# Edge features of a graph layer as three bf16 planes in one product, and loads for four groups at once

## The chip, the cores and the metric
One core of one Trainium2 chip. Time is device microseconds for one launch. The kernel before took 7721.66 us, the median of 3 runs (7720.5 to 7730.41).

## The reference, cut to what matters
12,500 nodes with 48 features, 400,000 edges sorted by target node, 16 features on each edge. Two layers, each with a residual. The first is a normalised graph convolution. The second, which the change touches, is a message network on edges:

```
h = relu(layernorm(x))
edge = concat(h[src], h[dst], edge_feat)           # 48 + 48 + 16
h1 = relu(edge @ W1 + b1)                          # 128
h2 = relu(h1 @ W2 + b2)                            # 128
message = h2 @ W3 + b3                             # 48
update = segment_sum(message, dst) / max(count, 1)
x = x + h + update
```

## The kernel before, in words
A first part (to about 2730 us) builds tables, does the graph convolution and writes p_tab and q_tab to HBM: for each node its share of the first layer, h @ W1[0:48] and h @ W1[48:96], each as three bf16 planes of 128 (768 bytes a row). The bf16 planes add up to nearly the f32 value.

The edge stage follows, and the change lies in it. The edges are padded to 401,408 = 784 groups (NG) of 512 (W = GROUP x P = 4 x 128). For group q:

- SyncE loads, for two groups at a time, source indices (idx), the edges' places within the target window (rel, broadcast to 96 partitions) and 16 rows of f32 edge features (ef, 16 of 128 partitions; the other 112 were cleared once, by memset, line 1454), and for each group 96 rows of q_tab (q_win, 32 nodes x 3 planes). A pair's loads wait until the first layer is done for all but 6 groups (`wait_past(sp, z1_made, q - (DEPTH - 2))`, DEPTH = 8).
- GpSimd gathers 4 x 128 rows of p_tab by four indirect DMAs (line 1362) into p_got, which has 4 buffers (UNROLL): it waits for the pair's loads and for z1_made to reach q - 3.
- VectorE makes two one-hots: hot_t (96 x 512, line 1530; it has two buffers and so waits for the first layer of group q-2) and hot_d (line 1534). ScalarE copies hot_d to bf16 (hot_c, line 1473).
- TensorE makes the first layer z1 (H x 512 in PSUM, two buffers) by the edge part (line 1322: w1c_sb, f32, 128 rows of which 112 are zero, 512 columns, recorded as two passes), the source part (line 1328: 12 bf16 products of 128 columns) and the target part (line 1495: one bf16 product of 96 rows and 512 columns, whose end tells z1_made).
- ScalarE applies bias and relu (h1, line 1348), TensorE multiplies by W2 (line 1334), VectorE keeps the maximum (h2, line 1352), TensorE sums by node (lines 1341 and 1343) and VectorE adds the sums up (lines 1357, 1358).

The order on TensorE is written out: in step q the first layer of q, the second layer of q-1, the sums of q-2. All five engines run a loop over 8 groups (`paced`), with one body per group, and meet only at semaphores. After the stage come rare extra groups (targets outside the 32-node window; `each_extra`) and a closing part with W3 and the division.

Of the kernel before, what the change touches and what calls it, by code (L numbers as in the profile page):

```python
# [17 lines left out]
P = 128  # L18
GROUP = 4
# [33 lines left out]
def paced(eng, steps, body, unroll=UNROLL):  # L53
# [6 lines left out]
    for s in range(unroll):  # L60
        body(steps - unroll + s, s)

# [66 lines left out]
def build_gnn(nc, x, src_col, dst_col, dst_row, edge_t, w0_t, b0, w1ab, w1c, b1, w2, b2, w3, b3, out):  # L129
# [40 lines left out]
    rel_row = dram("rel_row", [NG, W], BF16)  # L170

# [3 lines left out]
    with ExitStack() as whole:  # L175
# [34 lines left out]
        w1c_sb = sb("w1c_sb", [P, H], F32)  # L210
# [4 lines left out]
        w1c_zero = sem("w1c_zero")  # L215
# [465 lines left out]
        with ExitStack() as life:  # L681
# [10 lines left out]
            with ExitStack() as ctx:  # L692
# [26 lines left out]
                def _(pool):  # L719
                    link = linker(pool, scans)  # L720
                    pool.memset(w1c_sb[:, :], 0.0).then_inc(w1c_zero, 1)
# [21 lines left out]
                def _(sp):  # L743
# [38 lines left out]
                    sp.wait_ge(w1c_zero, 1)  # L782
                    weight(w1c_sb[0:EF, :], w1c)
# [536 lines left out]
        def edge_part(pe, z1, ef):  # L1320

            return pe.matmul(z1[:, :], w1c_sb[:, :], ef, start=True, stop=False, skip_group_check=True)  # L1322
# [44 lines left out]
        with ExitStack() as life:  # L1367
            PAIRS = DEPTH // 2
            PAIR_LOADS = 3
            idx = [sb(f"idx_d{j}", [P, 2 * GROUP], I32, life) for j in range(PAIRS)]  # L1370
            rel = [sb(f"rel{j}", [QR, 2 * W], BF16, life) for j in range(PAIRS)]
# [5 lines left out]
            rel_pairs = rel_row.rearrange("(g two) e -> g (two e)", two=2)  # L1377
# [7 lines left out]
            q_x = sb("q_x", [P, PLANES * H], BF16, life)  # L1385
            hot_x = p_flat[3][:, 0:W].rearrange("p (j e) -> p j e", j=GROUP)
# [10 lines left out]
            with ExitStack() as ctx:  # L1397
                ef_zero = sem("ef_zero", ctx)
                cnt_zero = sem("cnt_zero", ctx)
                pair_loaded = [sem(f"pair_loaded{j}", ctx) for j in range(PAIRS)]  # L1400
# [20 lines left out]
                def half_of(pair, s):  # L1421
                    width = pair.shape[1] // 2
                    return pair[:, s % 2 * width:(s % 2 + 1) * width]

                @block.sync
                def _(sp):
                    sp.wait_ge(ef_zero, 1)
                    sp.dma_start(cnt_acc[:, :], zero_b[:, 0:2 * NPP // P].bitcast(F32)).then_inc(cnt_zero, 16)

# [4 lines left out]
                    def step(q, s):  # L1434
                        if s % 2:
                            return
# [15 lines left out]
                def _(pool):  # L1452
                    for j in range(PAIRS):
                        last = pool.memset(ef[j][:, :], 0.0)
# [340 lines left out]
```

## Time and profile before
| what | value |
|---|---|
| median of 3 runs | 7721.66 us |
| the profiled execution: its span | 7782.5 us |
| TensorE busy, whole span | 6395.9 us (82%) |
| GpSimd busy | 3277.8 us (42%) |
| VectorE, ScalarE busy | 3430.9 us (44%), 1920.4 us (25%) |
| line 1322 (edge part) busy, 1568 passes | 1147.1 us |
| line 1362 (gathers) busy, 3136 of them | 2971.2 us |
| mean granted clock | 0.838 |

The profiled execution's own time is its span, 7782.5 us from first to last instruction; no other figure of it is given. The share of busy time is an average over stages with different limits. Idle time is put down to what ended it: "remote" is a semaphore whose updater the profile doesn't tell, "issue" is time in which the engine waited for nothing that the profile shows. Ends of TensorE's products are modelled, so distances are best taken from start to start.

### The profile page before, as it was taken

Reading aid. Unit: us, or ns where it says so; the run is one execution under the profiler, and the core shown is the slowest. Engines: PE = TensorE matmul, PEld = TensorE weight load, DVE = VectorE, ACT = ScalarE, POOL = GpSimd, SP = SyncE. Lnnn points to the kernel's source line nnn. Section 1 sums busy time; section 2 is a strip of 40 time slices with the busy share of each in tenths; the row PEclk is TensorE's granted clock in tenths of the full one; section 3 lists DMA queues with packets and bytes.
Section 4 is the critical chain, followed back from the end, with each engine's and each line's share of the span. In section 5 each row is a group of like instructions: output and inputs, shape, how many; then the busy total and the mean of one; then the engine's idle time right before and its main releaser. Section 6 shows DMA issues by size and latency. Waiting matters only on the chain. (4 is left out here: it accounts for less than half of the span.)

```text
span 7782.5 us, 170432 instructions
## 1 busy us (share of the span) xinstructions
PE 6395.9 (82%) x52124; PEld 5165.3 (66%) x52125; DVE 3430.9 (44%) x8786; ACT 1920.4 (25%) x3658; POOL 3277.8 (42%) x3414
## 2 busy tenths in 40 slices
PE   4868999999998777878888888888788888788878
PEld 4846878888777656666666666666666666666666
DVE  9989878888884612222222222222222222222222
ACT  1236555555541411111111111111111111111111
POOL 1020010001010255556555555555555555555565
PEclk9989999999999577788777778777878878778787
DMA  6026777777766333333333333333333333333333
GB/s 141 0 61 230 250 236 251 253 249 246 241 231 198 104 90 86 86 86 88 86 86 88 86 86 88 87 86 87 88 86 88 87 86 86 86 88 86 86 88 68
DMA packets 556929, 959.01 MB, mean 123 GB/s; under 512 B 277228, under 2 KB 356302, under 8 KB 556454
## 3 DMA queue, kind: packets, MB, share of 16 engines
q1 hardware_dynamic: 401687, 644.10, 26.4%
q0 software_dynamic: 155136, 313.54, 15.4%
q8 instruction: 62, 1.02, 0.1%
q14 instruction: 44, 0.36, 0.0%
HBM read 682.14 MB, written 275.03 MB: 123 GB/s over the span
## 5 line engine op out<-in xcount | busy, mean ns | idle before, releaser
L1362 POOL DMA_INDIRECT p_got<-p_tab,idx_d x3136 | 2971.2, 947 | 2015.1 <-remote 914.4
L1348 ACT ACTIVATE h<-z,b_col 128x512 f32<-128x512 f32 x784 | 538.7, 687 | 4040.1 <-remote 2909.2
L1352 DVE TENSOR_TENSOR h<-z,nb 128x512 f32<-128x512 f32 x784 | 538.7, 687 | 2169.2 <-remote 1522.9
L1334 PE MATMUL z<-w_sb,h 128*128 128x128 f32 x6272 | 1107.2, 312 | 397.1 <-issue 362.3
L1334 PEld LDWEIGHTS z<-w_sb,h 128*128 128x128 f32 x6272 | 1038.3, 226 | 510.3 <-issue 453.3
L816 PE MATMUL a_ps<-tile_r,pair_l 128*128 128x288 bf16 x6272 | 1228.8, 291 | 172.3 <-issue 84.9
L870 DVE TENSOR_SCALAR tile_r<-iota_r,key_r,dst_i 128x576 bf16<-128x576 f16 x3136 | 1171.2, 429 | 279.2 <-PE a_ps L816 133.7
L837 PE MATMUL out_ps<-gw,a_got 121*128 121x144 bf16 x13716 | 1259.3, 227 | 23.6 <-issue 13.1
L1341 PE MATMUL seg_ps<-hot_d,h 128*128 128x32 f32 x6272 | 965.5, 290 | 377.5 <-issue 374.1
L1341 PEld LDWEIGHTS seg_ps<-hot_d,h 128*128 128x128 f32 x6272 | 949.8, 222 | 428.1 <-issue 425.7
L796 ACT CAST stage<-a_ps 128x576 uint16<-128x576 f32 x1568 | 999.0, 638 | 874.3 <-PE a_ps L816 698.1
L1328 PEld LDWEIGHTS z<-ident_b,p_got 128*128 128x128 bf16 x9408 | 764.9, 117 | 650.1 <-issue 636.1
L1322 PE MATMUL z<-ef,w1c_sb 128*128 128x512 f32 x1568 | 1147.1, 821 | 30.1 <-DMA ef<-in_edge_t 24.1
L837 PEld LDWEIGHTS out_ps<-gw,a_got 121*128 121x128 fp8e4 x13716 | 1015.7, 98 | 152.8 <-issue 40.8
L1328 PE MATMUL z<-ident_b,p_got 128*128 128x128 bf16 x9408 | 841.5, 253 | 19.1 <-issue 9.9
L1357 DVE TENSOR_TENSOR big<-big,seg_ps 128x32 f32 x784 | 147.6, 188 | 1593.1 <-remote 1067.1
L727 POOL DMA_INDIRECT gw<-g_tab,gw_row x144 | 149.8, 1040 | 1601.0 <-PE out_ps L837 1559.7
L816 PEld LDWEIGHTS a_ps<-tile_r,pair_l 128*128 128x128 bf16 x6272 | 565.1, 115 | 310.8 <-ACT stage L796 147.8
L1495 PE MATMUL z<-hot_t_d,q_win 96*128 96x512 bf16 x784 | 360.7, 460 | 22.1 <-issue 21.5
L1322 PEld LDWEIGHTS z<-ef,w1c_sb 128*128 128x128 f32 x1568 | 289.3, 230 | 83.0 <-DMA ef<-in_edge_t 24.8
L1343 PE MATMUL seg_ps<-hot_c,ones_b 128*1 128x32 bf16 x3136 | 219.2, 179 | 150.8 <-issue 150.6
L1530 DVE TENSOR_SCALAR hot_t_d<-rel,node_id 96x512 bf16<-96x512 bf16 x784 | 310.2, 396 | 70.3 <-issue 49.8
(168 smaller groups left out, 3560.9 us busy)
## 6 DMA issues: line engine op xcount, KB each, us to landing
a_got<-a_tab SPq DMA_DIRECT2D x396, 576.0 KB, 4.0
a_tab<-stage SPq DMA_DIRECT2D x392, 576.0 KB
rel<-rel_row SPq DMA_DIRECT2D x392, 192.0 KB
p_got<-p_tab,idx_d POOLq DMA_INDIRECT x3136
ef<-in_edge_t SPq DMA_DIRECT2D x392, 64.0 KB
q_win<-q_tab SPq DMA_DIRECT2D x784, 24.0 KB
a_tab<-big SPq DMA_DIRECT2D x22, 567.0 KB
p_tab<-pq_out SPq DMA_DIRECT2D x14, 672.0 KB, 3.6
```

Source lines behind the costliest of these rows:

```text
L796: act.copy(stage[k][:, i % READ, :].rearrange("p (h e) -> p h e", h=2), a_ps[:, 2 * (i % 2):2 * (i % 2) + 2, 0:PIECE]).then_inc(kept, 1)
L816: last = pe.matmul(a_ps[:, 2 * (i % 2) + h, 0:PIECE], pair_l[i // 2 % 3][:, :, i % 2 * WIN_TILES + j], tile_r[i % 4 * WIN_TILES + j][:, h ...
L837: last = pe.matmul((a_ps if tail == 2 else out_ps)[:, c, b * OUT_F:(b + 1) * OUT_F], a_got[0:ROWS, i, :].bitcast(FP8)[:, (3 * c + b) * P:( ...
L870: dve.tensor_scalar(tile_r[i % 4 * WIN_TILES + j][:, :], iota_r[:, :], key_r[:, bass.ds(t, 1)], key_w[:, bass.ds(t, 1)], ALU.is_equal, ALU ...
L1322: return pe.matmul(z1[:, :], w1c_sb[:, :], ef, start=True, stop=False, skip_group_check=True)
L1328: pe.matmul(out_tile, p_rows[:, j, m * H:(m + 1) * H], ident_b[:, :], start=False, stop=False, skip_group_check=True)
L1334: last = pe.matmul(z2[:, j, :], h1_tile, w2_sb[:, :], start=True, stop=True)
L1341: pe.matmul(seg_ps[:, 0:nodes], h2[:, j, :], hot[:, j, :], start=(j == 0), stop=(j == GROUP - 1))
L1348: return act.activation(h1[:, :], z1[:, :], ACT.Relu, bias=b1_col[:, 0:1])
L1352: return dve.tensor_tensor(h2[:, :, :], z2[:, :, :], nb2[:, :].unsqueeze(1).to_broadcast([P, GROUP, H]), ALU.max)
L1362: pool.indirect_dma_start(p_rows[:, j, :], None, p_tab, bass.IndirectOffsetOnAxis(idx[:, j:j + 1], 0)).then_inc(landed, 16)
L1495: pe.matmul(z1[k][:, :], q_win[s][:, :], hot_t[k][:, :], start=False, stop=True, skip_group_check=True).then_inc(z1_made, 1)
```

## The change
Once, ahead of the stage, the 16 x 128 weights W1c are split into three bf16 planes: plane 0 is the rounded value, plane 1 the rounded rest, plane 2 the rest of that. Copies of the planes are laid on the 128 partitions of w1c_rows so that each edge plane meets the weight planes it needs: rows 0 to 47 meet edge plane 0 with weight planes 0, 1, 2; rows 48 to 95 edge plane 1 with 0, 1, 2; rows 96 to 127 edge plane 2 with 0, 1. The ninth product (2 with 2) sits in 16 more rows of the target part, which has 112 rows now: q_win gets the weight plane below its node rows, hot_t the edge plane below the one-hot.

The edge features are split on chip, 8 groups (a block) at a time, as 128 x 512 tiles: ScalarE rounds (three copies), VectorE subtracts (twice), SyncE saves the three planes to a new table e_tab in HBM and loads them back, with edge plane 0 and 1 to three places each and plane 2 to two and to hot_t. That runs up to two blocks ahead. Loads are for four groups (a set, two buffers) in place of two: six loads and four of node rows; they wait for all but 4 groups in place of all but 6. hot_t has room for 8 groups in place of two, and the wait ahead of it is relaxed. The extra groups keep the f32 product, now with 16 rows. The memsets go.

```diff
-            return pe.matmul(z1[:, :], w1c_sb[:, :], ef, start=True, stop=False, skip_group_check=True)
+            return pe.matmul(z1[:, :], weights, ef, start=True, stop=False, skip_group_check=True)
...
-            PAIRS = DEPTH // 2
-            PAIR_LOADS = 3
-            ef = [sb(f"ef{j}", [P, 2 * W], F32, life) for j in range(PAIRS)]
-            q_win = [sb(f"q_win{s}", [QR, H], BF16, life) for s in range(DEPTH)]
-            hot_t = [sb(f"hot_t_d{k}", [QR, W], BF16, life) for k in range(2)]
+            SET = 4
+            SETS = DEPTH // SET
+            SET_LOADS = 6
+            ER = QR + EF
+            e_rows = [(0, 3 * EF, 3), (3 * EF, 6 * EF, 3), (6 * EF, 8 * EF, 2)]
+            ef = [sb(f"ef{j}", [P, SET * W], BF16, life) for j in range(SETS)]
+            q_win = sb("q_win", [ER, DEPTH, H], BF16, life)
+            hot_t = [sb(f"hot_t_d{j}", [ER, SET * W], BF16, life) for j in range(SETS)]
...
+                    def load_block(n):
+                        sp.dma_start(e_left[:, :], block_view(n)).then_inc(e_loaded, 16)
+                    def save_block(n):
+                        sp.wait_ge(e_rounded, n * PLANES + PLANES)
+                        sp.sem_inc(sp_turns, 1)
+                        for m in range(PLANES):
+                            to = e_tab[m, :, bass.ds(n * (DEPTH * W), DEPTH * W)].rearrange("f (g e) -> f g e", g=DEPTH)
+                            sp.dma_start(to, e_planes[:, m, :]).then_inc(e_saved, 16)
...
-                        wait_past(sp, z1_made, q - (DEPTH - 2))
+                        wait_past(sp, z1_made, q - (DEPTH - SET))
...
+                        if s == 0:
+                            sp.wait_ge(e_saved, r * (16 * PLANES) + 16 * PLANES)
...
+                        for m, (low, high, copies) in enumerate(e_rows):
+                            sp.dma_start(ef[j][low:high, :], e_tab[m, :, cols].unsqueeze(1).to_broadcast([EF, copies, SET * W])
+                                         ).then_inc(set_loaded[j], 16)
+                        sp.dma_start(hot_t[j][QR:ER, :], e_tab[PLANES - 1, :, cols]).then_inc(set_loaded[j], 16)
+                        for i in range(SET):
+                            node_rows(q + i, s + i)
+                        if s == 0 and (not isinstance(r, int) or r + 1 < NG // DEPTH):
+                            save_block(r + 1)
+                            if not isinstance(r, int) or r + 2 < NG // DEPTH:
+                                load_block(r + 2)
...
+                    def round_block(n, m):
+                        if m == 0:
+                            act.wait_ge(e_loaded, n * 16 + 16)
+                            act.sem_inc(any_turn, 1)
+                            wait_past(act, e_saved, n * (16 * PLANES))
+                        else:
+                            act.wait_ge(e_taken, n * (PLANES - 1) + m)
+                        act.copy(e_planes[:, m, :], e_left[:, :]).then_inc(e_rounded, 1)
...
+                        if 1 <= s <= PLANES and (not isinstance(r, int) or r + 2 < NG // DEPTH):
+                            round_block(r + 2, s - 1)
                         act.wait_ge(hot_ready, q + 1)
...
-                        edge_part(pe, z1[k], half_of(ef[s // 2], s))
+                        edge_part(pe, z1[k], w1c_rows[:, :], set_part(ef[s // SET], s))
...
-                        wait_past(dve, z1_made, q - 1)
+                        wait_past(dve, z1_made, q - (DEPTH - 1))
...
+                        if 1 <= s < PLANES and (not isinstance(r, int) or r + 2 < NG // DEPTH):
+                            take_plane(r + 2, s - 1)
```

## Rows read from the trace of the kernel before

**Rows 1.** Windows, the edge stage: window, length, busy us (count), granted clock, DMA, GB/s
```profile
2730.00:7728.00 4998.00, 4020.60 (x27406) 3127.18 (x27407) 1175.33 (x3913) 714.36 (x1568) 2971.16 (x3136) 0.80 0.33 87
```

**Rows 2.** Groups by line, edge stage: count, busy us, mean ns, idle before, releasers
```profile
L1362 POOL DMA_INDIRECT p_got<-p_tab,idx_d x3136 | 2971.2, 947 | 2015.1 <-remote 914.4 <-issue 862.8 <-PE z L1495 232.0
...
L1348 ACT ACTIVATE h<-z,b_col 128x512 f32<-128x512 f32 x784 | 538.7, 687 | 4040.1 <-remote 2909.2 <-PE z L1495 1002.5 <-issue 93.6
```

**Rows 3.** Timeline of TensorE, one calm group: start, length, what, idle before
```profile
5003.22 1.13 PE L1322 MATMUL z<-ef,w1c_sb 128*128 128x512 f32 x2
...
5004.18 0.83 PE L1328 MATMUL z<-ident_b,p_got 128*128 128x128 bf16 x12
...
5004.85 0.38 PE L1495 MATMUL z<-hot_t_d,q_win 96*128 96x512 bf16 x1
5005.07 1.05 PE L1334 MATMUL z<-w_sb,h 128*128 128x128 f32 x8
...
5007.05 1.12 PE L1322 MATMUL z<-ef,w1c_sb 128*128 128x512 f32 x2
```

**Rows 4.** Timeline through a stall and the group after it
```profile
5016.35 0.38 PE L1495 MATMUL z<-hot_t_d,q_win 96*128 96x512 bf16 x1
...
5022.12 0.62 PE L1341 MATMUL seg_ps<-hot_d,h 128*128 128x32 f32 x2 [0.52 <-issue]
...
5027.24 2.08 PE L1322 MATMUL z<-ef,w1c_sb 128*128 128x512 f32 x2
5027.24 0.69 ACT L1348 ACTIVATE h<-z,b_col 128x512 f32<-128x512 f32 x1 [12.15 <-remote]
...
5029.11 1.49 PE L1328 MATMUL z<-ident_b,p_got 128*128 128x128 bf16 x12
...
5033.43 1.12 PE L1322 MATMUL z<-ef,w1c_sb 128*128 128x512 f32 x2
```

**Rows 5.** Timeline of GpSimd: gathers, with the idle time ahead of each
```profile
5002.13 0.94 POOL L1362 DMA_INDIRECT p_got<-p_tab,idx_d  x1 [1.90 <-PE z L1495]
...
5008.74 0.94 POOL L1362 DMA_INDIRECT p_got<-p_tab,idx_d  x1 [1.66 <-remote]
5011.39 0.94 POOL L1362 DMA_INDIRECT p_got<-p_tab,idx_d  x1 [1.70 <-issue]
...
5023.85 0.94 POOL L1362 DMA_INDIRECT p_got<-p_tab,idx_d  x1 [0.30 <-issue]
5028.02 0.94 POOL L1362 DMA_INDIRECT p_got<-p_tab,idx_d  x1 [3.23 <-remote]
...
5040.43 0.94 POOL L1362 DMA_INDIRECT p_got<-p_tab,idx_d  x1 [2.72 <-remote]
...
5047.02 0.94 POOL L1362 DMA_INDIRECT p_got<-p_tab,idx_d  x1 [1.91 <-remote]
...
5059.53 0.94 POOL L1362 DMA_INDIRECT p_got<-p_tab,idx_d  x1 [2.80 <-remote]
```

**Rows 6.** Timeline of SyncE's issues, and the window of a pair's loads beside gathers
```profile
5001.55 0.35 SPq L1441 DMA_DIRECT2D idx_d<-in_src_col  x1
...
5002.66 0.32 SPq L1445 DMA_DIRECT2D ef<-in_edge_t  x1
...
5002.90:5005.40 2.50, 2.50 (x24) 1.81 (x24) 0.97 (x5) 0.00 (x0) 1.89 (x3) 1.00 0.65 179
```

**Rows 7.** Timeline, start of the stage
```profile
2726.29 3.62 POOL L1454 MEMSET ef<- 128x1024 f32 x4 [26.57 <-POOLq L912]
...
2735.86 1.07 POOL L1362 DMA_INDIRECT p_got<-p_tab,idx_d  x1 [5.94 <-DMA ef<-in_edge_t]
...
2752.47 0.68 PE L1328 MATMUL z<-ident_b,p_got 128*128 128x128 bf16 x9 [1.65 <-DMA p_got<-p_tab,idx_d]
...
2754.30 0.22 PE L1328 MATMUL z<-ident_b,p_got 128*128 128x128 bf16 x1 [1.16 <-issue]
```

More of the change, by code:

```diff
@@ L61, in paced, with paced_ahead @@
         body(steps - unroll + s, s)
+def paced_ahead(eng, steps, body, unroll=UNROLL):
+    turns = steps // unroll
+    for s in range(unroll):
+        body(s, s, 0)
+    with eng.Fori(1, turns - 2) as r:
+        for s in range(unroll):
+            body(eng.snap(r * unroll + s), s, r)
+    for t in range(turns - 2, turns):
+        for s in range(unroll):
+            body(t * unroll + s, s, t)
 def wait_past(eng, sem, value):
@@ L1397, in build_gnn @@
             with ExitStack() as ctx:
-                ef_zero = sem("ef_zero", ctx)
                 cnt_zero = sem("cnt_zero", ctx)
-                pair_loaded = [sem(f"pair_loaded{j}", ctx) for j in range(PAIRS)]
+                set_loaded = [sem(f"set_loaded{j}", ctx) for j in range(SETS)]
+                e_loaded = sem("e_loaded", ctx)
+                e_rounded = sem("e_rounded", ctx)
+                e_taken = sem("e_taken", ctx)
+                e_saved = sem("e_saved", ctx)
+                w_rounded = sem("w_rounded", ctx)
+                w_taken = sem("w_taken", ctx)
+                w_placed = sem("w_placed", ctx)
                 q_loaded = [sem(f"q_loaded{s}", ctx) for s in range(DEPTH)]
@@ new lines, in _ @@
+                    load_block(0)
+                    sp.dma_start(cnt_acc[:, :], zero_b[:, 0:2 * NPP // P].bitcast(F32)).then_inc(cnt_zero, 16)
+                    sp.wait_ge(w_rounded, PLANES)
+                    for low, high, copies in e_rows:
+                        sp.dma_start(w1c_rows[low:high, :], w1c_planes[:, 0:copies, :]).then_inc(w_placed, 16)
+                    sp.dma_start(q_win[QR:ER, :, :], w1c_planes[:, PLANES - 1:PLANES, :].to_broadcast([EF, DEPTH, H])
+                                 ).then_inc(w_placed, 16)
@@ L1451, in _ @@
                 @block.gpsimd
                 def _(pool):
-                    for j in range(PAIRS):
-                        last = pool.memset(ef[j][:, :], 0.0)
-                    last.then_inc(ef_zero, 1)
                     def step(q, s):
-                        pool.wait_ge(pair_loaded[s // 2], slot_count(q, s, 16 * PAIR_LOADS))
+                        pool.wait_ge(set_loaded[s // SET], set_count(q, s))
                         pool.sem_inc(pool_turns, 1)
@@ L1468, in _, with step @@
                 def _(act):
-                    def step(q, s):
+                    def round_block(n, m):
[6 more added lines that the diff above has]
+                        act.copy(e_planes[:, m, :], e_left[:, :]).then_inc(e_rounded, 1)
+                    for m in range(PLANES):
+                        wait_past(act, w_taken, m)
+                        act.copy(w1c_planes[:, m, :], (w1c_left if m else w1c_sb)[:, :]).then_inc(w_rounded, 1)
+                    for n in range(2):
+                        for m in range(PLANES):
+                            round_block(n, m)
+                    def step(q, s, r):
+                        if 1 <= s <= PLANES and (not isinstance(r, int) or r + 2 < NG // DEPTH):
+                            round_block(r + 2, s - 1)
                         act.wait_ge(hot_ready, q + 1)
@@ L1494, in first @@
                         pe.wait_ge(q_loaded[s], slot_count(q, s, 16))
[L1495 removed]
+                        pe.matmul(z1[k][:, :], q_win[:, s, :], set_part(hot_t[s // SET], s), start=False, stop=True,
                                   skip_group_check=True).then_inc(z1_made, 1)
```

91 lines of the change are left out of this document (55 added, 36 removed).

## The prediction
> **What bounds the kernel now.** I read first where the time lies, then who is held in that stretch, then the order of events. The edge stage, 784 groups of 512 edges, takes 4998 us of 7782.5 (2730 to 7728), so 6.37 us for a group; TensorE is busy in 4020.6 us of it, at a mean granted clock of 0.80 [rows 1]. That looks like a TensorE bound, and the product that the change shrinks (line 1322) is its dearest. The timeline says it is only half true. In a calm stretch TensorE needs 5007.05 - 5003.22 = 3.83 us for a group [rows 3]. GpSimd issues four gathers for a group, each 0.947 us busy with 0.30 us ahead of it [rows 2, 5]: 4 x 1.247 = 4.99 us. So TensorE at the full clock is already faster than GpSimd, and neither explains 6.37.
>
> The missing time is in stalls. In [rows 4] the last product of a group starts at 5016.35, yet the activation that waits for it alone (its neighbours being done) starts at 5027.24, and in between TensorE starts its queued work piece by piece, with 0.5 us and more of idle time ahead of each that nothing releases ("issue"). GpSimd alone keeps its pace. ScalarE's 2909 us of "remote" waits [rows 2] are the sum of such hold-ups. The stall ends when the gathers do: the last of a run starts at 5023.85, ends at 5024.79, and everything moves again at 5027.2; GpSimd resumes at 5028.02 [rows 4, 5]. I don't know the mechanism. The trace shows only that a stall comes some way into an unbroken run of gathers (here 5 us, from 5011.39 to 5016.35; in others that I followed up to 9), and that it lasts until the run is over and has landed. It comes too where TensorE itself waits for gathers: at the start of the stage GpSimd runs from 2735.86 without a break, TensorE waits for a gather at 2752.47, and is in the steps of a stall (1.16 us of idle time ahead of one product) by 2754.30 [rows 7].
>
> GpSimd breaks off because a gather for group q waits for the first layer of group q-4 (four buffers). From 5002.13 to 5059.53 it does 9 groups, 6.38 us each, as the mean. Its rows with more than the usual 0.30 us of idle time are the six of [rows 5]: three of 1.66 to 1.91 us, most of them where TensorE is slow after a stall, and three of 2.72 to 3.23 us, each the end of a stall. Over the usual gap they make 12.2 us for 9 groups, 1.36 us each: 4.99 + 1.36 = 6.35. So the stage is GpSimd's gathers plus the breaks in them, and the change is worth what it takes from the breaks.
>
> **The change, part by part.**
> Edge product. Two f32 passes (5003.22 to 5004.18, 0.96 us) become one bf16 product of 512 columns, which line 1495 shows: 5005.07 - 5004.85 = 0.22 us [rows 3]. At the lower clock (1.2 GHz, granted 0.5) the f32 passes take 5029.11 - 5027.24 = 1.87 us [rows 4], and the bf16 product, at half the speed, twice 0.22, 0.44 us (an estimate). A group falls from 3.83 to 3.09 us in calm, and from 6.19 (5027.24 to 5033.43) to 4.76 after a stall. That is 0.74 to 1.43 us a group, 580 to 1121 us over 784; as a gain it would count in full only if TensorE set the pace. It doesn't: 4.99 us stands above both new figures.
>
> The breaks. After the change even a slow TensorE group (4.76) is under 4.99, so the three short breaks go: by [rows 5] 1.66 + 1.70 + 1.91 less 0.90 is 4.4 us in 9 groups, 0.48 us a group. But without them GpSimd's runs become longer, and a run over some 5 to 9 us brings a stall whose end costs 2.92 us, 2.62 over the usual gap. How long can a run get? GpSimd may go on for each first layer that TensorE has reported before the stall. Until about 7 us into the run TensorE, resuming slowly, now does two for certain and sometimes a third (first after 1.5 to 2 us, then 4.7, then 3.1). So a run is two or three groups: 4.99 + 2.62/2 = 6.30, or 4.99 + 2.62/3 = 5.86. I take the middle, 6.08: 784 x (6.37 - 6.08) = 227 us less. The bounds of this term: 4.99 + 0.1 (no stalls, -1000 us) and 6.37 (0).
>
> Loads. For four groups at once there are six loads in place of two times three, and the edge planes go out three and two times over. Per group in KB: rel 96 as before, edge rows 32 before, now 131 + 16, and in addition 33 of f32 read and 49 written for the table; with node rows and indices about 154 before and 350 now. Gathers are 393. At 6.1 us that is 122 GB/s against 87 [rows 1]; the same engines moved 179 GB/s in a stretch with both kinds [rows 6]. The mean fits. Cost in the mean 0; the bounds come with the burst (below): 0 to +1.5 us a group. By the Trainium skill's page "DMA: Bandwidth & Descriptors", section "Queues, rings and completion order", each DMA engine takes turns between the queues at packet granularity, which speaks against the change: during a set's 983 KB the gathers would lose part of their share. The sum above has no term for it; rows 6 show 179 GB/s for both together, but not who gave way.
>
> Lead of the loads. SyncE now waits for all but 4 groups instead of all but 6, while GpSimd may start group q at all but 3. If GpSimd is at its greatest lead, the release that lets SyncE load set q also lets it start group q-1, 4.99 us before it needs the set. Six issues at (5002.66 - 5001.55)/2 = 0.56 us are 3.3 us; 983 KB at 179 GB/s, or at the 100 that gathers (98 KB in 1.247 us, 79 GB/s) leave, are 5.5 to 9.8 us [rows 6]. So 9 to 13 us against 4.99: up to 4 to 8 us every four groups. In a run, however, GpSimd is one or two groups behind that lead, and the wait shrinks to 0 to 3 us; and a wait is also a break that puts off a stall. I take 0.03 us a group, 24 us.
>
> Rounding. ScalarE makes three copies of 128x512 per 8 groups, VectorE two subtractions. The nearest row is the 128x512 activation, 687 ns [rows 2]: 0.26 us a group on ScalarE, 714 us busy of 4998, and 0.17 on VectorE, 1175 busy [rows 1]. The copy stands ahead of the activation of its group: 0.69 + 0.29 + 0.69 = 1.7 us, under the 3.09 between two first layers. Behind a late block (its load, or the saving of the one before) hot_c and the activation would queue, and TensorE's second layer after them; both were issued some 4 groups earlier, about 20 us. Cost 0; without that cover 2 to 3 us per 8 groups, 290 us at the most. Waits for buffers of hot_t fall away on VectorE; it was not on the path, 0.
>
> Start. Before, memsets of 3.62 us and 5.9 us of loads lead to the first gather [rows 7]. Now: load (3 us), three roundings with two subtractions and hand-overs (5), three saves (5), six loads and landing (8), some 21 us against 9.6: +11 us, between +5 and +25.
>
> **Sum.** 7782.5 - 227 + 24 + 11 = 7590 us for the profiled span. The median of the runs, 7721.66, is 0.992 of the profiled span, 61 us below it; scaled so, 7530. I take 7520.
>
> **Rivals.**
> A. Runs end without stalls. If the stall needs TensorE's dense f32 work beside the gathers, GpSimd runs through: about 5.1 us a group, 784 x 1.27 = 996 us less, 6790 + 11, about 6750 scaled. For it: stalls begin after TensorE's densest stretches. Against it: [rows 7].
> B. The load wait takes over, and the kernel is slower. Place: GpSimd's wait for set_loaded, every fourth group. It decides from the point where a set lands over about 6 us after GpSimd wants it (1.36 us a group of breaks now, times four, is 5.4 us). SyncE's issues fall into the stalls, where they too go in steps, which stretches the 3.3 us; then SyncE needs the stall's end, loads for 9 us or more, and GpSimd stands. Per four groups 20 + 8 = 28 us, 7.0 a group: +494, about 8210; halfway, 6.65, it is 7940. For it: the shorter lead. Against: a standing GpSimd ends the stall and lets TensorE use its four full buffers.
> C. Nothing left. Always two-group runs and a little load wait: 6.30 to 6.45, 7680 to 7800. TensorE's saved time is then spent waiting in the stall.
> That the product isn't cheaper is no rival: rows of line 1495 have its shape.
>
> **Numbers.** Forecast (5.6 to 6.25 us a group, 7160 to 7650) 0.50; A 0.13; C 0.13; B 0.24. A measurement of this kernel tells about 0.2%, 15 us, from no change. Faster: 0.50 + 0.13 + 0.04 of C = 0.67; same 0.06; slower 0.24 + 0.03 = 0.27. The range 7000 to 7860 leaves out most of A and the dearer half of B. Its own range for the likeliest case is 7160 to 7650.
>
> **What would show it.** The first layer's product at 0.22 us, and TensorE's busy time in the stage down by over 800 us, while the stage falls by far less; GpSimd's idle sum (2015 us) down by some 200, with its breaks of about 1.7 us gone and those of about 2.9 us more often than one in three groups. ScalarE's "remote" waits stay near 2900 us or grow. Wrong would be: those waits mostly gone (A), or GpSimd released mainly by the loads of the set (B).

## The result, and the profile after

The changed kernel takes 8007.91 us (median of 4 runs, 7997.41 to 8018.94) against 7721.39 (4 runs, 7720.5 to 7730.41): a ratio of 1.0369, 95% interval 1.0356 to 1.0383, so 3.7% slower where 2.6% faster was forecast. Its profiled execution has a span of 8007.0 us and a mean granted clock of 0.78. The first gather starts at 2746.9 us (2735.9 before, [rows 7]), 11 us later, and the rest is lost in the stage: from there 6.62 us a group in place of 6.36. (The 11 us are between two profiled executions whose chips aren't known to be the same. On one chip the changed kernel with loads in pairs starts its first gather at 2740.5 us, g1_lead4, and the kernel before with four buffers of hot_t at 2734.5, g4_four_hot4; on another e1_pairs starts at 2746.2 and three kernels made from the one before at 2741.5 to 2744.4. So with loads in pairs the start costs 2 to 6 us; what sets of four add to it was not timed on one chip.)

The window of the edge stage (columns as in [rows 1]):

```profile
2770.00:7940.00 5170.00, 3649.67 (x26480) 3139.69 (x26481) 1260.20 (x4084) 859.86 (x1846) 2973.09 (x3118) 0.71 0.44 112
```

TensorE is busy 0.706 of it, against 0.804 in [rows 1]: the work was taken away and the stage grew. Its busy time fell by 371 us only (4020.6 to 3649.7), where the edge product alone fell by 773 (1147.1 to 374.2), since the other products took longer at a granted clock of 0.71 in place of 0.80. Here is the dearest of them, the product with W2, before and after:

```profile
L1334 PE MATMUL z<-w_sb,h 128*128 128x128 f32 x6264 | 1106.1, 312 | 397.1 <-issue 362.3 <-DVE h L1352 22.9 <-ACT h L1348 6.0
...
L1345 PE MATMUL z<-w_sb,h 128*128 128x128 f32 x6232 | 1266.6, 346 | 466.8 <-issue 447.9 <-DVE h L1363 7.6 <-ACT h L1359 3.4
```

The groups by line in the stage after (as in [rows 2]; the last is the product that replaced line 1322):

```profile
L1373 POOL DMA_INDIRECT p_got<-p_tab,idx_d x3118 | 2973.5, 954 | 2195.4 <-issue 861.3 <-remote 750.9 <-DMA hot_t_d<-e_tab 489.3
...
L1359 ACT ACTIVATE h<-z,b_col 128x512 f32<-128x512 f32 x780 | 536.1, 687 | 4126.7 <-remote 3397.4 <-PE z L1575 571.6 <-issue 88.1
...
L1333 PE MATMUL z<-ef,w1c_rows 128*128 128x512 bf16 x779 | 374.2, 480 | 59.5 <-issue 58.6
```

Two things are new against [rows 2]. GpSimd is released for 489 us by the landing of a set's loads, which did not stand there before, and ScalarE's "remote" idle time is 3397 in place of 2909 us. The waits of the same window of the changed kernel give the counts (total us, times, longest):

```profile
ACT h L1359 <- remote: 3397.4, 392, 20.2
...
POOL p_got L1373 <- remote: 750.9, 282, 4.5
...
POOL p_got L1373 <- DMA hot_t_d<-e_tab: 489.3, 110, 8.3
```

TensorE's calm group, to be laid beside [rows 3]: start to start 3.10 us (5000.67 to 5003.77), the edge product 0.23:

```profile
5000.67 0.39 PE L1333 MATMUL z<-ef,w1c_rows 128*128 128x512 bf16 x1
...
5000.90 0.83 PE L1339 MATMUL z<-ident_b,p_got 128*128 128x128 bf16 x12
...
5003.77 0.39 PE L1333 MATMUL z<-ef,w1c_rows 128*128 128x512 bf16 x1
```

And GpSimd's breaks, beside [rows 5], with SyncE's issues of one set beside [rows 6]:

```profile
5001.24 0.95 POOL L1373 DMA_INDIRECT p_got<-p_tab,idx_d  x1 [1.89 <-remote]
...
5013.48 0.94 POOL L1373 DMA_INDIRECT p_got<-p_tab,idx_d  x1 [2.54 <-remote]
...
5022.29 0.94 POOL L1373 DMA_INDIRECT p_got<-p_tab,idx_d  x1 [4.11 <-DMA hot_t_d<-e_tab]
...
5040.73 0.94 POOL L1373 DMA_INDIRECT p_got<-p_tab,idx_d  x1 [3.75 <-remote]
...
5049.46 0.94 POOL L1373 DMA_INDIRECT p_got<-p_tab,idx_d  x1 [4.04 <-DMA hot_t_d<-e_tab]
```

```profile
5012.71 0.69 ACT L1359 ACTIVATE h<-z,b_col 128x512 f32<-128x512 f32 x1 [9.23 <-remote]
...
5013.06 0.36 SPq L1498 DMA_DIRECT2D idx_d<-in_src_col  x1
...
5014.16 2.39 SPq L1503 DMA_DIRECT2D ef<-e_tab  x3
...
5017.30 0.01 SPq L1505 DMA_DIRECT2D hot_t_d<-e_tab  x1
...
5019.48 3.79 SPq L1485 DMA_DIRECT2D q_win<-q_tab  x4
```

A stall ends at 5012.7; only then SyncE is told of the first layer, and issues the set from 5013.06. GpSimd, released by the same signal, does the last group that it has indices for (four gathers from 5013.48) and stands until the set has landed; it goes on at 5022.29, 9.2 us after SyncE's first issue. That is the new wait. After it come a calm stretch of TensorE and the next stall.

Over the whole stage I took every gather's idle time ahead of it, and call over 0.5 us a break. Sums are over the usual 0.30 us; "SyncE" is the mean time from the start of the first issue of a set's (or pair's) loads to the end of the last.

| kernel (on the chip of its run) | us a group | breaks | their sum, us | under 2.2 us | 2.2 to 3 | over 3 | SyncE, us |
|---|---|---|---|---|---|---|---|
| before | 6.36 | 536 | 1052 | 261 | 260 | 15 | 6.8 |
| after | 6.62 | 435 | 1247 | 77 | 123 | 235 | 12.4 |
| e1_pairs | 6.49 | 519 | 1132 | 222 | 151 | 146 | 9.5 |
| e3_cheap | 6.32 | 488 | 1015 | 176 | 307 | 5 | |
| f1_noround | 6.28 | 464 | 987 | 128 | 333 | 3 | 8.2 |
| g1_lead4 | 6.61 | 484 | 1234 | 163 | 153 | 168 | 9.6 |
| i2_saves | 6.39 | 501 | 1076 | 200 | 231 | 70 | 8.6 |
| i3_saves_wait | 6.51 | 525 | 1164 | 224 | 109 | 192 | 10.0 |
| h3_saves_wait, another chip | 5.03 | 0 | 0 | 0 | 0 | 0 | 6.2 |

Of after's 235 breaks over 3 us, 160 stand at the first of a set's four groups; all breaks there make 708 of the 1247 us. The rows come from several chips, and that alone moves them: the unaltered change on another chip (i1_after) has 441 breaks with a sum of 1313 us (82, 78 and 281 of the three sizes). Differences of some 60 us in the sums say little by themselves; the ratios below, each against the kernel before on its own chip, decide.

### The profile page after: what moved, and what is told of

Read it like the earlier page. It is cut to its first block and busy times, and to the rows that moved or that the text cites. A ratio compares the mean times of both kernels' runs of the same rounds, so it can differ in the third digit from the quotient of the medians.

```text
span 8007.0 us, 170913 instructions
## 1 busy us (share of the span) xinstructions
PE 6049.8 (76%) x51340; PEld 5197.2 (65%) x51341; DVE 3526.8 (44%) x8984; ACT 2077.3 (26%) x3955; POOL 3293.6 (41%) x3409
## 5 line engine op out<-in xcount | busy, mean ns | idle before, releaser
L1345 PE MATMUL z<-w_sb,h 128*128 128x128 f32 x6272 | 1274.5, 346 | 467.2 <-issue 447.9
L1345 PEld LDWEIGHTS z<-w_sb,h 128*128 128x128 f32 x6272 | 1195.0, 258 | 625.2 <-issue 561.4
L1352 PE MATMUL seg_ps<-hot_d,h 128*128 128x32 f32 x6272 | 1045.8, 303 | 441.9 <-issue 433.7
L1352 PEld LDWEIGHTS seg_ps<-hot_d,h 128*128 128x128 f32 x6272 | 1048.6, 241 | 477.6 <-issue 475.7
L1339 PE MATMUL z<-ident_b,p_got 128*128 128x128 bf16 x9408 | 957.2, 264 | 335.5 <-issue 286.5
L1339 PEld LDWEIGHTS z<-ident_b,p_got 128*128 128x128 bf16 x9408 | 803.3, 120 | 558.2 <-issue 458.4
L1333 PE MATMUL z<-ef,w1c_rows 128*128 128x512 bf16 x784 | 377.1, 481 | 93.6 <-issue 58.6
L1575 PE MATMUL z<-hot_t_d,q_win 112*128 112x512 bf16 x784 | 400.2, 510 | 52.6 <-issue 51.1
L873 DVE TENSOR_TENSOR pair_l<-rows_b,key_l 128x512 bf16<-128x512 bf16 x784 | 329.2, 420 | 14.1 <-PEq L300 11.8
L1622 DVE TENSOR_SCALAR hot_t_d<-rel,node_id 96x512 bf16<-96x512 bf16 x784 | 289.7, 369 | 46.3 <-issue 39.3
```

Source lines behind the costliest of these rows:

```text
L1333: return pe.matmul(z1[:, :], weights, ef, start=True, stop=False, skip_group_check=True)
L1339: pe.matmul(out_tile, p_rows[:, j, m * H:(m + 1) * H], ident_b[:, :], start=False, stop=False, skip_group_check=True)
L1345: last = pe.matmul(z2[:, j, :], h1_tile, w2_sb[:, :], start=True, stop=True)
L1352: pe.matmul(seg_ps[:, 0:nodes], h2[:, j, :], hot[:, j, :], start=(j == 0), stop=(j == GROUP - 1))
L1575: pe.matmul(z1[k][:, :], q_win[:, s, :], set_part(hot_t[s // SET], s), start=False, stop=True, skip_group_check=True).then_inc(z1_made, 1)
```

## The experiments

Ratios are to the kernel before, run beside it on the same chip; in brackets the 95% interval. Kernels whose name begins with the same letter shared a chip and their runs of before (7795.76 us for e, 7716.17 for f, 7718.39 for g, 6605.17 for h, 7802.11 for i); f and g ran on one chip, so there are four. Where ratios of different letters are subtracted below, 0.2 points are not told from nothing.

### Which part of the change costs

**e1_pairs**: the change with loads for two groups and the old lead of six.

```diff
-            SET = 4
+            SET = 2
```


> The kernel after, but with loads for two groups at once (four buffers of a set, SyncE again waits for all but 6 groups); planes, table and one bf16 product stay. Theory L (the late loads of a set cost the time, and the bf16 product itself gains what the forecast said): GpSimd is released by the landing of a set no more (489 us before, under 50 now), the stage falls to 6.0 to 6.3 us a group, the kernel to 7450 to 7700 us. Rival S (the stalls take back what TensorE saves, whatever the loads do): 7700 to 7900 us, ScalarE's remote waits stay above 3000 us. Rival D (the added traffic of the planes is the cost): 7900 us or more.

1.0156 (1.0139 to 1.0173), 7911.09 us. GpSimd's time released by the loads falls from 489 to 0.3 us, and 2.1 of the 3.7 points go. The rest stays, so the late sets are not the whole loss, and the cheap product's gain doesn't come to light behind them.

**e2_four**: the kernel before with loads for four, nothing else.

```diff
-            PAIRS = DEPTH // 2
+            PAIRS = DEPTH // 4
...
-                        wait_past(sp, z1_made, q - (DEPTH - 2))
+                        wait_past(sp, z1_made, q - (DEPTH - 4))
```


> The kernel before, with nothing changed but loads for four groups at once (two buffers of a set, three loads and four of node rows, SyncE waits for all but 4 groups). The set is 648 KB against 983 in the kernel after. Theory L: GpSimd waits some 2 to 4 us every four groups for the set, 7850 to 8200 us, with 300 to 500 us of GpSimd released by a load. Rival S: the waits only take the place of the breaks at a stall's end, 7700 to 7800 us.

0.9961 (0.9947 to 0.9975). By itself the grouping costs nothing, with its shorter lead: three loads and four of node rows land in time (29 us of waits for them in all). The short lead costs with the change's larger loads, not with these.

**g1_lead4**: e1_pairs with the lead alone cut from six to four.

```diff
-                        wait_past(sp, z1_made, q - (DEPTH - SET))
+                        wait_past(sp, z1_made, q - (DEPTH - 4))
```


> e1 (the kernel after with loads for two groups) with one number changed: SyncE waits for all but 4 groups, as in the kernel after, not all but 6. It parts the late start of the loads from the size of a set. Theory L (the lead is what makes the set late): 7990 us or more on the chip where e1's ratio was 1.016, so a ratio of 1.03 or more, with GpSimd released by a load for 300 us or more. Rival B (the burst of a set of four is the cost): a ratio of 1.01 to 1.02.

1.0348 (1.0328 to 1.0369). This one line gives 1.9 of the 2.1 points (g1_lead4 and e1_pairs ran on different chips), and brings the changed kernel's wait back, in pairs, with its size:

```profile
POOL p_got L1373 <- DMA hot_t_d<-e_tab: 427.5, 105, 7.5
```

**g4_four_hot4**: e2_four with four buffers of hot_t, the change's looser wait on VectorE.

```diff
-                        wait_past(dve, z1_made, q - 1)
+                        wait_past(dve, z1_made, q - 3)
```


> e2 (the kernel before with loads for four groups) with four buffers of hot_t in place of two, so that VectorE waits for the first layer of four groups back, not two. It is the other part of the change that needs no planes. If VectorE's wait for TensorE's held signal is on the path: a ratio of 0.985 to 0.993 against e2's 0.996. If not: 0.995 to 0.998.

0.9970 (0.9960 to 0.9980), level with e2_four: that wait was not on the path.

**e3_cheap**: the kernel before with a bf16 product of 96 rows in place of the edge part.

```diff
-                        edge_part(pe, z1[k], half_of(ef[s // 2], s))
+                        pe.matmul(z1[k][:, :], ident_b[0:QR, :], half_of(rel[s // 2], s), start=True, stop=False,
+                                  skip_group_check=True)
```


> The kernel before, but the edge part is one bf16 product of 96 rows and 512 columns (an identity times the loaded rel) in place of the f32 product with the edge features; the features are still loaded but don't enter. It shows what the cheap product alone is worth. Theory L and the forecast: 6.08 us a group, 7500 us (7250 to 7650). Rival S: within 1% of 7721 us, because the stalls grow by what TensorE saves. Rival A of the prediction (stalls need the f32 product): 6750 us, ScalarE's remote waits nearly gone.

0.9963 (0.9945 to 0.9981). This is all that the cheap product is worth: 0.4 points, some 29 us (36 between the medians; one of the ten runs took 7822 us), where the prediction counted 580 to 1121 off TensorE. Short breaks fall from 261 to 176, but those of 2.2 to 3 us rise from 260 to 307, and the sum falls by 37 us only. Here is a short break of this kernel, ACT's activation waiting for the product of line 1496:

```profile
5023.36 0.63 PE L1496 MATMUL z<-hot_t_d,q_win 96*128 96x512 bf16 x1
...
5024.47 0.95 POOL L1362 DMA_INDIRECT p_got<-p_tab,idx_d  x1 [0.30 <-issue]
...
5026.49 0.69 ACT L1348 ACTIVATE h<-z,b_col 128x512 f32<-128x512 f32 x1 [4.87 <-remote]
...
5027.27 0.94 POOL L1362 DMA_INDIRECT p_got<-p_tab,idx_d  x1 [1.86 <-remote]
```

The product starts at 5023.36 and is a single one. Its effect is seen at 5026.49, 1.07 us after GpSimd's last gather has ended (5025.42). TensorE was not late; its signal was, until the gathers were done. This short break is a held signal like the long ones.

Not every one is. A gather that waits for TensorE waits for one known product, the last of the first layer four groups back, so each break can be laid beside the start of its product. In the kernel before, 100 of the 228 short breaks at a group's start end within 2.5 us of that start: there TensorE was late, and these breaks sum to 137 us over the usual gap. (The other 33 of the 261 stand inside a group, where GpSimd waits for no semaphore.) In e3_cheap there is none of them, and the shortest such distance is 2.9 us. But the other breaks at a group's start rose from 403 (869 us) to 461 (977 us). So the cheap product does take away the breaks that TensorE caused, and the stalls take most of it back. The counts are from different chips: f3_thin, with the old product, has 96 of the late ones, e2_four only 30.

**f1_noround**: e1_pairs without the round trip per block; every group reads the planes of the first block.

```diff
-                        cols = bass.ds(q * W, SET * W)
+                        cols = bass.ds(s * W, SET * W)
...
-                            save_block(r + 1)
-                                load_block(r + 2)
-                            round_block(r + 2, s - 1)
-                            take_plane(r + 2, s - 1)
```


> As e1 (the kernel after with loads for two groups), but only the first block of edge features is loaded, rounded and saved; every set loads the planes of that block again, so the edge features of later groups are the wrong ones. What is left out is the round trip per block: 4 DMAs, three copies, two subtractions. Theory S (stalls take back TensorE's saving, and what is added on the DMA side and in front of the activation is paid in longer breaks): between 7700 and 7850 us where e1 had 7911, if the round trip is half or more of e1's 1.6%. Rival W (the loads of the planes three and two times over are the cost): 7870 to 7920, no gain.

1.0014 (1.0004 to 1.0024). So 1.4 points hang on the round trip; the planes' four loads in place of one of f32 and the later start leave 0.5 beside e3_cheap.

**g2_engonly**: f1_noround with ScalarE's copies and VectorE's subtractions again, on stale data.

```diff
+                        if 1 <= s <= PLANES and (not isinstance(r, int) or r + 2 < NG // DEPTH):
...
+                            act.copy(e_planes[:, s - 1, :], e_left[:, :]).then_inc(e_rounded, 1)
...
+                            take_plane(r + 1, s - 1)
```


> f1 (planes of the first block only) with the three copies and two subtractions per 8 groups put back, on stale data, but no load or save of a block (not the reference's result). f1's ratio was 1.001, e1's with the whole round trip 1.016. Theory E (the copies ahead of the activation and the subtractions ahead of the one-hots cost): 1.010 or more. Rival W (the DMAs of the round trip and SyncE's place in the queue cost): 1.000 to 1.005.

1.0005 (0.9995 to 1.0014): they cost nothing.

**i2_saves** (its expectation also names h1_saves, the same kernel on another chip): f1_noround with the three saves per block, no wait.

```diff
+                        if s == 0 and (not isinstance(r, int) or r + 1 < NG // DEPTH):
+                            for m in range(PLANES):
...
+                                sp.dma_start(to, e_planes[:, m, :]).then_inc(e_saved, 16)
```


> The kernel of h1_saves again. With stalls: f1_noround was at 1.0014 and the whole round trip (e1_pairs) at 1.0156; if the three saves cost by traffic or by their place in SyncE's queue, 1.008 to 1.016; if the wait for them or the block's load costs, 1.000 to 1.003. Without stalls: 1.002 again.

**i3_saves_wait**: i2_saves with the change's addresses and its wait.

```diff
-                        cols = bass.ds(s * W, SET * W)
+                        cols = bass.ds(q * W, SET * W)
...
+                            sp.wait_ge(e_saved, r * (16 * PLANES) + 16 * PLANES)
```


> The kernel of h3_saves_wait again: i2_saves with SyncE's wait for the saves and the loads at fresh addresses. With stalls: if these cost, 0.4% or more over i2_saves; if the saves alone do it, level with it within 0.2%. Without stalls: 1.002 again.

i2_saves 1.0034 (1.0021 to 1.0046), i3_saves_wait 1.0160 (1.0143 to 1.0177). The saves cost 0.2 points beside f1_noround on another chip, which is no more than the noise; this last edit costs 1.3 on one chip, nearly the whole of the round trip. The wait for saved planes releases nothing in the trace (no row of SyncE names it), so by the trace it is the loads from a register's address, at fresh places in the table; no run has the wait or the addresses alone. What they do is to be seen on SyncE, whose idle time ahead of a set is its slack (first i2_saves, then i3_saves_wait, both from 2770 to 7600 us):

```profile
SPq L1492 <- remote: 613.7, 171, 9.8
SPq L1492 <- PE z L1572: 399.9, 139, 6.1
```

```profile
SPq L1492 <- remote: 345.3, 156, 8.8
SPq L1492 <- PE z L1572: 85.7, 47, 4.3
```

1014 us of slack become 431 (f1_noround: 1375), and a pair's issues take 10.0 us in place of 8.6, where a pair of groups has 13. The trace shows where the time goes: from the end of rel's issue to the end of the third issue of ef SyncE takes 3.49 us in place of 1.86, with 9 of its instructions in place of 3, as the address of each load is now worked out in a register; on the chip without stalls (below) the same step is 2.36 in place of 1.94. No run parts that arithmetic from the reading of fresh data. The trace doesn't show how that lengthens the breaks; SyncE is late, yet GpSimd's waits are put down to "remote", not to a load.

**i1_after**: the changed kernel, unaltered, on this chip.

> The change itself, unaltered. If the chip has no stalls (before near 6605 us): GpSimd's gathers without a break, 5.03 us a group as in h3_saves_wait, and only the later start is left, +0.2% (1.001 to 1.005); if the short lead of sets of four costs there too, 1.02 or more, with GpSimd released by the set's loads. If it has stalls (before near 7720): 1.035 to 1.039 again.

1.0369 (1.0352 to 1.0386), 8085.68 us against 7802.11: the result again on a chip where both kernels take 1% longer.

### What the stalls hang on

**f2_noload**: the kernel before, without SyncE's loads after the first 8 groups.

```diff
-                        sp.dma_start(idx[j][:, :], src_col[:, bass.ds(q * GROUP, 2 * GROUP)]).then_inc(pair_loaded[j], 16)
...
+                            sp.sem_inc(pair_loaded[j], 16 * PAIR_LOADS)
```


> The kernel before, but SyncE loads only for the first 8 groups; later it only counts the semaphores on, so indices, windows, features and node rows are those of the first 8 groups (the result is not the reference's). If the stalls come from gathers alone: same pattern, ScalarE's remote waits above 2000 us, 7400 to 7800 us. If SyncE's loads beside the gathers bring them: remote waits under 500 us, GpSimd runs through at 5.0 us a group, 6700 us.

0.9876 (0.9857 to 0.9896). The loads cost 1.2 points in all (the gathers fetch the rows of the same 8 groups throughout, which is in that number too), and the stalls stay. From 2770 to 7600 us, where the kernel before has 2819:

```profile
ACT h L1348 <- remote: 3356.4, 391, 12.8
```

**f3_thin**: gathered rows of 256 bytes in place of 768.

```diff
-                pool.indirect_dma_start(p_rows[:, j, :], None, p_tab,
+                pool.indirect_dma_start(p_rows[:, j, 0:H], None, p_tab.rearrange("n (m h) -> (n m) h", m=PLANES),
```


> The kernel before, but each gathered row is 256 bytes in place of 768 (other rows; TensorE uses the one plane three times; not the reference's result). Gathers are as many and take GpSimd as long. If a stall comes from the bytes or the packets in flight: it goes or comes much later in a run, remote waits under 1500 us and under 7300 us. If it comes from GpSimd's making of the gathers (128 rows each, a run without a break): the same pattern, remote waits above 2400 us, 7600 to 7800 us.

0.9997 (0.9987 to 1.0008). A third of the bytes, the same pace and the same time; ACT's "remote" waits from 2770 to 7600 us are 2818 us, those of the kernel before 2819. Neither bytes nor traffic make the stalls.

**e4_drain**: GpSimd waits for the last group's gathers to land before it issues the next.

```diff
+                        if past(q, 1):
+                            pool.wait_ge(gathered[(s - 1) % DEPTH], slot_count(q - 1, (s - 1) % DEPTH, 16 * GROUP))
+                            pool.sem_inc(pool_turns, 1)
```


> The kernel before, but GpSimd waits before the gathers of a group until those of the group before have landed, so that no run of gathers is longer than four. If the stalls come from unbroken runs of gathers they go: ScalarE's remote waits fall from 2909 us to under 500, TensorE needs 3.83 us a group where it isn't waiting, and the stage is GpSimd's 4.99 + 1.5 to 1.9 us a group, 6.5 to 6.9, so 7800 to 8100 us. If they come from something else (TensorE's rate, SyncE's loads), the remote waits stay above 1500 us and the time is above 8100.

1.0963 (1.0945 to 1.0982), 8544 us. That is over the 7800 to 8100 expected: 818 breaks of 2.5 us cost more than the stalls did. But with them the stalls are gone: the "remote" rows of ACT have left the list, and what remains is waiting for TensorE, itself waiting for gathers:

```profile
ACT h L1348 <- PE z L1498: 3809.7, 583, 8.7
POOL p_got L1362 <- DMA p_got<-p_tab,idx_d: 1688.8, 660, 3.2
PE z L1328 <- DMA p_got<-p_tab,idx_d: 1156.3, 568, 4.6
```

**f4_gap**: a register read on GpSimd ahead of every second gather.

```diff
             for j in range(GROUP):
+                if j % 2:
+                    pool.value_load(extra_total[0:1, 0:1], min_val=0, max_val=NB * NG)
```


> The kernel before, but GpSimd reads a register from memory ahead of every second gather (some 0.3 to 0.5 us), so its gathers are thinner in time though the queue never empties: 5.6 to 6 us a group in place of 4.99. If density is what brings a stall: stalls come later or not, remote waits under 1500 us, 7200 to 7600 us. If only an empty queue ends them (as in e4): runs stall as before and the added time is added to the runs, 8000 to 8300 us.

1.0064 (1.0048 to 1.0081), and it decides nothing: gathers in a run stay 1.25 us apart, so the read didn't thin them.

**g3_gap4**: four such reads ahead of every gather.

```diff
+                for _ in range(4):
+                    pool.value_load(extra_total[0:1, 0:1], min_val=0, max_val=NB * NG)
```


> The kernel before, with four register reads ahead of each gather, since one ahead of every second changed nothing in GpSimd's pace: I expect 1.5 to 1.7 us from gather to gather in place of 1.25. If it is the density of gathers that brings the stalls: remote waits of ScalarE under 1000 us and 6.0 to 6.8 us a group, 7500 to 8150 us. If any unbroken run brings them: remote waits above 2000 us and 7.5 us a group or more, 8500 us or more.

1.5306 (1.5276 to 1.5337). Gathers are mostly 2.67 us apart, not the 1.5 to 1.7 expected, a group takes 11.5 us, and the times expected are both missed. What decides is that no "remote" waits of ACT are left here either:

```profile
ACT h L1348 <- PE z L1497: 4469.8, 421, 15.2
```

Together: on these chips the stalls need the unbroken run of gathers at 1.25 us (e4_drain, g3_gap4). They need neither the other loads (f2_noload), nor the bytes (f3_thin), nor the f32 edge product (e3_cheap). At which spacing between 1.25 and 2.67 us they end, and whether it is the spacing or the landing of each gather before the next, is open.

### A chip without stalls

**h1_saves**, **h2_loads**, **h3_saves_wait**: f1_noround with the saves, with the block's load, and with saves, wait and fresh addresses (edits as in i2_saves and i3_saves_wait; h2_loads issues `load_block(r + 1)` every 8 groups).

> f1_noround (loads for two groups, no round trip, planes of the first block in every group) with the three saves of a block's planes issued again every 8 groups, without a wait ahead of them; what is saved is stale. f1_noround was at 1.0014, the whole round trip (e1_pairs) at 1.0156. If the saves cost by their traffic or by their place in SyncE's queue, between 1.008 and 1.016. If the cost is the wait for them, or the block's load, 1.000 to 1.003.

> f1_noround with the load of a block's f32 edge features (128 x 512, 256 KB) issued again every 8 groups; nothing reads them. If this load costs, 1.005 to 1.012; if not, 1.000 to 1.003. The saves are three times as many transfers of half the bytes each, so by traffic alone the load would be 0.4 of the round trip's cost, 1.007.

> h1_saves with the loads at the addresses that the saves wrote (a new block every 8 groups, in place of the first one always) and SyncE's wait for the last block's saves ahead of them, as the change has it; the planes saved are those of the first block. If wait or fresh addresses cost, this lies over h1_saves by 0.4% or more; if the saves alone do it, level with h1_saves within 0.2%. With h2_loads' excess added it should come to e1_pairs' 1.0156.

They ran on a chip on which the kernel before takes 6605.17 us, 14% less than on the others (24 runs, 6601.48 to 6610.84), and gave 1.0023, 1.0023 and 1.0022 (all within 1.0013 to 1.0033). GpSimd's line of h1_saves, and h3_saves_wait's waits below it:

```profile
L1373 POOL DMA_INDIRECT p_got<-p_tab,idx_d x3136 | 2992.9, 954 | 999.1 <-issue 900.4 <-PE z L1572 54.2 <-DMA hot_t_d<-e_tab 44.5
```

```profile
ACT h L1359 <- PE z L1572: 3034.6, 728, 7.2
...
PEld z L1339 <- DMA p_got<-p_tab,idx_d: 864.0, 417, 4.3
...
POOL p_got L1373 <- issue: 851.0, 2793, 0.3
```

The longest wait of GpSimd in the stage is 0.3 us: not one break in 3136 gathers, 5.03 us a group, TensorE waiting for gathers, no "remote" wait. The stage is what [rows 2, 5] give for GpSimd alone. The same program at the same pace (0.95 + 0.30 us) brings 501 breaks on the other chip (i2_saves, 7829.68 us) and none on this one (h1_saves, 6621.40). Not all of that lies in the edge stage: the first gather starts at 2753.6 us there and at 2599.8 here. The edit that costs 1.3 points with stalls costs nothing here (1.0023 to 1.0022), and SyncE issues the same pair's loads in 6.2 us where it took 10.0 in i3_saves_wait: its issues are themselves drawn out by the stalls. So the expectations of h1_saves to h3_saves_wait, written for a chip with stalls, could not be decided here, and i2_saves and i3_saves_wait put the question again. The 0.2% over before (15 us) is in part a later start (first gather 6 us later in f1_noround than in [rows 7]). The whole change was not timed on this chip, so what its short lead does there is open.

## Why the prediction was wrong

**Right: what bounds the stage.** GpSimd's gathers plus the breaks in them, and TensorE hardly. e3_cheap takes the product out and gets 0.4%; the stall-free chip shows the bare 5.03 us a group beside the 4.99 worked out.

**Right: the sizes of single steps.** Edge product 0.23 us (0.22 forecast), calm group 3.10 (3.09), rounding 0 (g2_engonly), hot_t's buffers 0 (g4_four_hot4). The first gather is 11.0 us later (+11 forecast), but that agreement may be luck: with loads in pairs, on one chip, it is 2 to 6. Of e3_cheap's groups 146 take 4.5 to 4.9 us start to start on TensorE, near the 4.76 forecast after a stall, though 101 take 5.5 to 5.9. TensorE lost 0.73 us in a calm group and the stage gained next to none of it.

**Failed: "even a slow TensorE group (4.76) is under 4.99, so the three short breaks go", worth 227 us.** It needed TensorE's slowness to be their cause. It is that of 100 of 261, 137 us, and those did go; e3_cheap, where nothing but the product is changed, kept 176 short breaks and gained 29 us. The rest at a group's start are held signals: the signal of a product that was in time passes only when the gathers are over. And its runs became 1.61 groups long (784 by 488), from 1.46, in place of the two or three forecast. In the changed kernel the short breaks did go (261 to 77), but their place was taken by 220 more of over 3 us.

**Failed: "Lead of the loads", taken at 0.03 us a group, 24 us.** The estimate of the set itself was good: 9 to 13 us were forecast and 9.2 is read above. What was wrong is the choice that "GpSimd is one or two groups behind that lead". The stall holds SyncE's release back too, so both start from the same signal, with one group's indices in hand (4.99 us) against 9.2. g1_lead4 against e1_pairs prices it: 1.9 points, about 150 us, or 0.19 us a group. The upper bound, 1.5, held it; the value in the sum was over six times too small.

**Failed: the loads, "Cost in the mean 0".** Larger loads and later start cost 0.5 points together (f1_noround against e3_cheap), saves 0.2, loads at fresh addresses with their wait 1.3: some 150 us in all. I had reckoned bytes per second, and what the runs point to is SyncE's time to issue: 6.8 us a pair before, 10.0 in i3_saves_wait, of 12.7 to 13 that there are. That this time is the cause is argued, not shown. The page "DMA: Bandwidth & Descriptors" of the Trainium skill (section "Queues, rings and completion order"), which the prediction weighed, has each DMA engine take turns between queues packet by packet. No run here shows the gathers losing by it: GpSimd issues them at 0.95 + 0.30 us in a run under 87, 112 and, on the chip without stalls, 142 GB/s; how fast each one lands was not measured.

**The signs.** Two that were named failed with the sum. TensorE's busy time was to fall by over 800 us and fell by 371, as the other products ran longer at the lower granted clock (0.71 for 0.80). GpSimd's idle sum was to fall by some 200 us and rose from 2015 to 2195. The product at 0.23 us, the short breaks mostly gone (261 to 77) and ScalarE's "remote" waits above 2900 us came as said.

**The rivals.** B was the one that came: its place (GpSimd's wait for set_loaded) and its halfway case (6.65 us a group, 7940 us) are nearly what was measured (6.62, 8008). (Halfway between 6.37 and 7.0 is 6.69, not 6.65, so about 7970 us.) But B carries only about half of the loss; the other large part, the loads at fresh addresses, is named nowhere in the prediction. A (5.1 us a group, 6750 us) is how one chip behaves with every kernel that ran there, before included, and e3_cheap shows that the stalls don't need the f32 product. The range ended at 7860, since it left out the dearer half of B.

**The sum**, in points (terms from different chips put together): cheap product -0.4; larger loads and later start +0.5; saves +0.2; fresh-address loads +1.3 (with rounding, e1_pairs is 1.0156); lead from six to four +1.9; sets of four +0.2, which is what is left over. Together 3.7.

**What stays open.** What inside the chip holds signals and instructions back during a run of gathers, and why one chip doesn't. Why the loads at fresh addresses lengthen the breaks. No kernel here that computes the same takes more than 0.4% off the one before (e2_four 0.9961, g4_four_hot4 0.9970).

## What to carry to other kernels

Before pricing a cheaper product, ask who sets the pace: here 0.73 us off a calm group of TensorE was worth 0.04 us a group. Before crediting it with the breaks of the engine that does, lay each break beside the start of the product it waits for: 100 of 261 short ones were TensorE's. When loads are made larger and their lead shorter in one edit, set the time from the release to the landing (9.2 us) against what the consumer has in hand at that same release (4.99 us), and count the issuing engine's time per set, not only bytes. And where much of the time is in waits that the profile can't name, run before and after on several chips: a seventh of this kernel's time was a matter of which chip it ran on.

## What the runs showed of the hardware

- On every chip here but one, indirect gathers at 1.25 us each, unbroken, delay other engines' instructions and signals from some 4 us on (in the changed kernel a run starts at 5001.24, and TensorE's queued products go singly from 5005.42), until the gathers are over. With a wait for landing after every four (e4_drain), or at 2.67 us each (g3_gap4), they don't. They need not be large: 256-byte rows do it as 768-byte rows do (f3_thin).
- The delay depends on the chip: one and the same kernel has 501 breaks on one (i2_saves) and none on another (h1_saves), and the kernel before takes 7716, 7796 and 7802 us on three chips and 6605 on a fourth.
- An indirect gather of 128 rows costs GpSimd 0.95 us plus 0.30, with rows of 768 bytes and of 256 (947 ns both, f3_thin). One register read ahead of every second one leaves the distance at 1.25 us (f4_gap), four ahead of each add 1.42 us (g3_gap4).
- In a stall SyncE is slowed too: the same issues for a pair take 10.0 us on a chip with stalls (i3_saves_wait) and 6.2 on the one without (h3_saves_wait).
- Less work on TensorE brought a lower granted clock: 0.80 over the stage before [rows 1], 0.71 after, 0.72 in e3_cheap (2770 to 7600 us). It stood idle for over 0.5 us 1147 times (1223 us in all) in the stage after, against 751 times (731 us).
